# Rewriting a quantised feed-forward kernel: style fetch, roundings, statistics in pairs and the place of the x work

## The reference

```python
w = weights[conditions]                        # (32, 32, 32)
z = einsum('bct,bcd->bdt', x, w)               # style mixing of channels
def rmsnorm(x, g): return g * x * rsqrt(mean(x*x, -1) + 1e-8)
def act_quant(x):
    scale = 127 / clip(max(abs(x), -1), 1e-4)
    return clip(round(x * scale), -128, 127) / scale
def ternary(w):
    s = mean(abs(w))
    return round(tanh(w / (s + 1e-8))) * arctanh(s)
def linear(x, w, g): return act_quant(rmsnorm(x, g)) @ ternary(w).T
h = silu(linear(z, w1, g1)) * linear(z, w2, g2)     # 1024 hidden
out = x + linear(h, w3, g3)
```

## Time and profile before

| | |
|---|---|
| time, median of 3 runs | 78.19 us (77.08, 78.45, 78.19) |
| the profiled execution: span from first to last instruction | 76.6 us |
| what lies around the span, against the median | 1.6 us |
| DVE, POOL, PE, ACT busy | 58.1, 55.4, 48.0, 47.7 us |
| mean granted TensorE clock | 0.889 |

### The profile page before, as it was taken

How to read it: one execution, slowest core, us unless ns; L and a number is a source line. 1 busy time by engine, 2 the same in 40 slices (tenths; PEclk the granted TensorE clock), 3 DMA queues, 4 the chain that set the end, 5 groups by cost and what they waited for, 6 DMA issues and landing times.

```text
span 76.6 us, 1068 instructions
## 1 busy us (share of the span) xinstructions
PE 48.0 (63%) x298; PEld 31.3 (41%) x302; DVE 58.1 (76%) x117; ACT 47.7 (62%) x70; POOL 55.4 (72%) x97
## 2 busy tenths in 40 slices
...
GB/s 0 119 385 346 327 237 278 330 210 115 253 71 0 0 0 4 0 9 4 0 0 0 0 0 4 17 52 9 68 0 68 0 68 0 23 45 0 68 68 68
DMA packets 5369, 6.22 MB, mean 81 GB/s; under 512 B 500, under 2 KB 4980, under 8 KB 5364
## 3 DMA queue, kind: packets, MB, share of 16 engines
...
q0 software_dynamic: 256, 0.13, 0.8%
...
HBM read 5.11 MB, written 1.05 MB: 80 GB/s over the span
## 4 chain that ended last, share of the span: by engine, by line
DVE 24%; issue 22%; POOL 22%; DMA 12%; PE 11%; ACT 4%; SPq 0%; POOLq 0%; DVEq 0%
DMA w_sb<-in_L_ffn_w 12%; POOL hg L325 11%; PE y_ps L769 6%; DVE xg L477 6%; DVE cw_diag L446 5%; DVE x_peak L482 5%; PE a_ps L652 3%; PE t_ps L758 2%; POOL h_deq L302 2%; DVE hid L551 2%; ACT hr L413 2%; DVE abs_sum L438 2%; POOL h_root L316 2%; POOL h_base L311 2%; POOL h_base L309 1%
## 5 line engine op out<-in xcount | busy, mean ns | idle before, releaser
L325 POOL TENSOR_TENSOR hg<-hid,g_all 128x1024 f32<-128x1024 f32 x7 | 16.5, 2358 | 0.8 <-DVE hid L551 0.8
L413 ACT ACTIVATE hr<-hg,rounder,h_scale 128x1024 f32<-128x1024 f32 x7 | 8.7, 1241 | 5.5 <-DVE h_scale L574 5.5
L769 PE MATMUL y_ps<-w_t,hq_t 128*128 128x256 bf16 x64 | 10.3, 319 | 2.1 <-DVE hq_t L581 2.0
L560 DVE TENSOR_REDUCE h_peak<-hg 128x1 f32<-128x1024 f32 x8 | 9.7, 1217 | 1.7 <-POOL hg L325 1.6
L551 DVE SCALAR_TENSOR_TENSOR hid<-v_ps,x_deq,gate 128x1024 f32<-128x1024 f32 x8 | 10.2, 1271 | 0.9 <-PE v_ps L725 0.6
L725 PE MATMUL v_ps<-w_t,xq_t 128*128 128x512 bf16 x30 | 8.9, 415 | 3.0 <-DVE hid L551 2.9
L399 ACT ACTIVATE gate<-a_ps,x_deq 128x1024 f32<-128x1024 f32 x8 | 8.8, 1100 | 2.2 <-PE a_ps L725 2.1
L725 PE MATMUL a_ps<-w_t,xq_t 128*128 128x512 bf16 x30 | 8.7, 407 | 1.8 <-issue 1.3
L218 POOL DMA_INDIRECT cw_rows<-in_L_cond_weights,row_idx x8 | 7.9, 982 | 2.4 <-issue 2.1
L769 PEld LDWEIGHTS y_ps<-w_t,hq_t 128*128 128x128 bf16 x64 | 6.9, 115 | 5.6 <-DVE hq_t L581 4.1
L652 PE MATMUL a_ps<-x_sb,cw_diag 128*128 128x256 f32 x16 | 7.0, 597 | 2.5 <-DVE cw_diag L446 2.5
...
## 6 DMA issues: line engine op xcount, KB each, us to landing
...
cw_rows<-in_L_cond_weights,row_idx POOLq DMA_INDIRECT x8, 4.3
cond_i<-in_itok_B SPq DMA_DIRECT2D x1, 0.1 KB
```

Source lines behind the costliest of these rows:

```text
L325: pool.tensor_tensor(hg[:, b], hid[:, b], g3_all[:], ALU.mult).then_inc(hg_ready, 1)
L413: act.activation(hr[:, t % 2], hg[:, t % 2], ACT.Identity, scale=h_scale[:, t % 2:t % 2 + 1], bias=rounder[:]).then_inc(hr_ready, 1)
L560: dve.tensor_reduce(h_peak[:, b], hg[:, t % 2], AX.X, ALU.max, apply_absolute_value=True).then_inc(hpeak_ready, 1)
L769: last = pe.matmul(y_ps[t % 2][:, 0:FEAT], hq_t[:, t % 2, j, :], w_t[2][:, j, :], start=(j == 0), stop=(j == KH - 1))
```

## The change

Nearly every engine's list is written anew. By part:

- Style weights. SP reads the 32 style numbers into registers and issues, for each sequence, a transfer of its 32x32 matrix (4 KB) straight onto the diagonal of cw_diag: eight for each pair, between the loads of w3, x2, x3 and g3. The row numbers, gathers and diagonal copies go. DVE fills cw_diag with zeros. ACT issues the loads of w1, g12, w2 and x1 before its first arithmetic.
- Weight rounding. tanh and the rounding pass are one multiplication by 1/(2 arctanh(1/2) s), written to int16 (which rounds); the copy from PSUM clips to -1..1 (DVE) or takes the sign (ACT).
- Activation rounding. x and h are multiplied by the scale into int16 instead of adding a large number in float32; transposes read them dense, and the copies read int16 from PSUM.
- Statistics. eps comes in as an extra column of the squared tensor, so one power -0.5 gives the inverse root. For h, power, reciprocal, scale and factor are made for two tiles at once. hg has four buffers.
- x work. ACT copies the conditioned x from PSUM to SBUF (xc), DVE multiplies by g1 and POOL by g2. The x work of pairs 2 and 3, the transpose and copy of pair 1, and w3's rounding and turn stand behind the first silu. arctanh's steps move from POOL to DVE.
- The last tile's gain, rounding and copy are halved between two engines.

```diff
 @block.sync
+            load_x(sp, 0)
+            _, style = nc.values_load_multi_w_load_instructions(
+                cond.rearrange("(o b) -> o b", o=1), engines=[mybir.EngineType.SP], min_val=0, max_val=STYLES - 1,
...
+            def fetch(p):
+                for b in range(2 * p * PER_TILE, 2 * (p + 1) * PER_TILE):
+                    t, s = b // PER_TILE, slice(b % PER_TILE * CHAN, (b % PER_TILE + 1) * CHAN)
+                    sp.dma_start(cw_diag[s, t, s], cond_w[bass.ds(style[b], 1)].rearrange("o c d -> (o c) d")
+                                 ).then_inc(cw_in[p], 16)
+            sp.wait_ge(diag_zero, 1)
+            fetch(0)
+            load_w(sp, 2, 0)
+            fetch(1)
+            load_w(sp, 2, 1)
+            load_x(sp, 2)
+            fetch(2)
+            load_x(sp, 3)
+            fetch(3)
             sp.dma_start(g3_all[:], g3.partition_broadcast(P)).then_inc(g3_in, 16)
 @block.gpsimd
+            def x_gain(p):
+                pool.wait_ge(xc_copied, p + 1)
+                pool.tensor_tensor(xg[:, p, 1], xc[:, 2 * p:2 * p + 2, 0:FEAT],
+                                   g12[:, 1, :].unsqueeze(1).to_broadcast([P, 2, FEAT]), ALU.mult).then_inc(xg_p, 1)
+            def x_quant(p, k, i):
+                pool.wait_ge(xscale_ready, p + 1)
+                pool.tensor_scalar(xq[:, p, k, i], xg[:, p, k, i], x_scale[:, p, k, i:i + 1], 1.0,
+                                   ALU.mult, ALU.mult).then_inc(xq_done[p], 1)
+            def w_quantise(m, h):
+                pool.wait_ge(inv_ready, m + 1)
+                pool.tensor_scalar(half_of(m, h, w_q), half_of(m, h, w_sb), w_inv[:, m:m + 1], 1.0,
+                                   ALU.mult, ALU.mult).then_inc(w_quant[m][h], 1)
+            def inverse_rms(lo, hi):
+                pool.wait_ge(hss_ready, hi)
+                pool.tensor_tensor(h_rms[:, lo:hi], h_ss[:, lo:hi], neg_half[:, 0:hi - lo], ALU.pow
+                                   ).then_inc(hrms_ready, hi - lo)
```

More of the change, by code:

```diff
@@ L7 @@
 FP16 = mybir.dt.float16
[L8 to L9 removed]
+INT16 = mybir.dt.int16
 ALU = mybir.AluOpType
@@ L630, in _ @@
-            peak_of(last)
-            step_of(last)
-            scale_of(last)
-            rounding_last(last)
-            keep_h(last - 1)
-            residual(last - 2)
-            keep_h(last)
-            residual(last - 1)
-            residual(last)
+            abs_sum_half(0, 1)
+            mean(0)
+            w_quantise(0, 0)
+            w_quantise(0, 1)
+            keep_w(0, 0)
+            x_gain(0)
+            mean(1)
+            keep_w(0, 1)
+            x_peak_of(0)
+            x_scales(0)
@@ new lines, in _ @@
+            x_quant(0, 0, 0)
+            x_quant(0, 0, 1)
+            w_quantise(1, 0)
+            x_gain(1)
+            keep_w(1, 0)
+            x_keep(0)
+            mean(2)
+            arctanh_in()
+            x_peak_of(1)
+            x_scales(1)
+            arctanh_out()
+            hidden(0)
+            x_gain(2)
+            hidden(1)
+            x_keep(1)
+            peak_of(0)
+            x_peak_of(2)
+            x_scales(2)
+            hidden(2)
+            peak_of(1)
@@ new lines, in _ @@
+            scales(0, 2)
+            keep_w(2, 0)
+            x_gain(3)
+            hidden(3)
+            x_keep(2)
+            keep_h(0)
+            peak_of(2)
+            x_peak_of(3)
+            x_scales(3)
+            keep_h(1)
+            hidden(4)
+            residual(0)
+            x_keep(3)
+            peak_of(3)
+            scales(2, 4)
+            residual(1)
+            hidden(5)
+            keep_h(2)
+            peak_of(4)
+            keep_h(3)
+            hidden(6)
@@ L772, in _ @@
+                done.then_inc(y_ready, 1)
+            total(0)
+            pe.wait_ge(ident_made, 2)
+            condition(0)
+            w_turn(0, 0)
+            w_turn(0, 1)
+            total(1)
+            condition(1)
+            x_turn(0)
+            w_turn(1, 0)
+            w_turn(1, 1)
+            total(2)
             up_a(0)
             up_v(0)
-            x_turn(2)
-            x_turn(3)
-            for t in range(TILES):
-                if t + 1 < TILES:
-                    up_a(t + 1)
-                if t >= 3:
-                    down(t - 3)
-                if t + 1 < TILES:
-                    up_v(t + 1)
-                if t == 0:
-                    w_turn(2, 0)
-                    w_turn(2, 1)
-                if t >= 2:
-                    h_turn(t - 2)
```

875 lines of the change are left out of this document (407 added, 468 removed).

## The result

The changed kernel takes 94.78 us (median of four, 94.53 to 97.22) where the kernel before takes 78.0: a ratio of 1.227, with a 95% interval of 1.217 to 1.237. The forecast was 83.6 us in a range of 73.5 to 90. The direction was right and the size was not: it lies 4.8 us above the range. The profiled execution has a span of 92.8 us at a mean granted clock of 0.848; before it was 76.6 at 0.889, so 16.2 us came on top. Some executions of most kernels here take a few per cent longer than the rest, at a lower granted clock (97.22 us is one, at 0.833); the medians contain them, the ratios and intervals leave them out.

What follows compares the result with a forecast made beforehand. POOL was taken to bound the loop, 4.0 us a tile, with DVE 0.4 us behind. silu(0) at 28.4 plus 53.6 behind it gave 82.0 us of span; with 1.6 to the median, 83.6 us, range 73.5 to 90.

Steps and rivals of the forecast that it cites:

- Register reads: Ahead of silu(0), SP reads 32 style numbers into registers: 4.2 us taken, between 1.5 and 11.8.
- The chain from condition(0) to silu(0): Ahead of the loop: pair 0's transfers land at 10.2 us, then steps in written order, silu(0) at 28.4.
- In-order lists: Loop: x_turn(2) ahead of up_v(2) idles DVE 3.7 us before hidden(2); a second stall, 2.4 us, at residual(0).
- Rival 1: Loop: the walked stalls are filled and DVE's own work bounds; 74.0 us, chance 0.25.
- rival 2: Half of the packing: hidden(2) at 10.5 us after silu(0), prologue at 27.7; some 77.5 us, chance 0.10.
- The port: DVE and POOL exclude each other with two SBUF inputs: nothing taken for small operands or x_gain, 2.4 us at worst.
- a row with x_step beside a POOL pow: Kernel before: x_step, with two small SBUF inputs, ran its 0.15 us without a pause; small operands priced at nothing.
- TensorE's clock: Loop with long waits may get the lower level, 1.2 GHz, doubling some ten steps of 0.6 to 0.9 us.
- rival 3: Registers at 11.8 us or slower TensorE, either adding 7.6: 91 us; chance 0.15 together with slow int16 reads.
- Durations: Instruction times: ACT's rounding 1.15 us, int16 PSUM copies 0.68, DVE's weights 0.75, x_quant 0.47, gain 2.36, POOL's x_gain 1.18.
- Rival 4: DVE reads int16 PSUM at the reduce's rate, 8 us more: 88 to 92 us; chance within a shared 0.15.
- Chances: Whole kernel: faster by over 2% 0.24, within 2% 0.13, slower 0.63.

Runs made afterwards that it cites:

- the three parts together: Changed kernel with registers read in four portions, h's scale by per-partition pointer, and x_turns and x_quants behind what the current tile needs: 86.9 us, ratio 1.127.
- The best order tried for the new lists: Changed kernel with the x work back ahead of hidden(0), registers read in four portions and h's scale by pointer: 85.84 us, ratio 1.119.

## Why the prediction was wrong, by its steps

The sum was 82.0 us of span; it was 92.8. Of the 10.8 us, 5.6 lie ahead of silu(0) (33.98 for 28.4) and 5.2 behind it (58.8 for 53.6). The steps that failed are three terms: the reads, taken at 4.2 us, took 10.07; the lock on h's scale, taken at nothing, took 2.2; and TensorE's lower clock, left out of the walk, took some 3. The direction came from the lists' order, and that step held.

- **Register reads: the largest step that failed.** They were taken at 4.2 us, between 1.5 and 11.8, and took 10.07; the transfers of pair 0, forecast to land at 10.2, let condition(0) start at 16.32. With no transfer beside them they take 4.27 us; that this is so near the 4.2 is luck, as the middle of two guesses 8 times apart. What was left out is that other transfers run just then, 2 MB of weights among them; no such interaction is in the sum, though the upper end of the bounds held. Missing too is the read of the array's address, 1.71 us of the 10.07. The Trainium skill, page "Runtime: NRT & Kernel Launch", section "Instruction fetch mechanics", gives some 200 ns a register: measured were 0.13 without other transfers and 0.31 with them, on either side of it (0.10 and 0.25 without the address).
- **The chain from condition(0) to silu(0)** was walked at 18.2 us and took 17.7. Right.
- **In-order lists: right, and the core of the forecast's direction.** x_turn(2) ahead of up_v(2) gave 3.70 us of idle DVE in front of hidden(2) (3.7 forecast), 14.15 us after silu(0) (13.2), and the second stall came at residual(0). That order decides was then shown by moving only names in the lists: 7.1 us, of which the clock's part was not measured by itself. Rival 1 (packed) and rival 2 (half) are out by this.
- **The port: taken at nothing, with 2.4 us at worst.** The first scale of h took 2.35 us in place of 0.16, the third (78.75 us) 0.57, and hidden(3) started 20.4 us after silu(0) and not 17.4; of these 3.0 us 0.95 were there at hidden(2), the other 2.05 are the lock. I had let a row with x_step beside a POOL pow speak for small operands in general. It speaks for no more than that pair of instructions. In the changed kernel a pow meets the lock too: the one at 53.89, begun 0.11 us behind DVE's x_gain, took 1.13 us and not 0.70. The Trainium skill, page "SBUF — State Buffer", section "Who interferes with whom", states the rule without an exception for small operands, and beside a gain the trace agrees with it (2.35 us).
- **TensorE's clock: in rival 3, with 15% for three things together, and outside the forecast.** Between 48 and 63 us the granted clock is 0.67 and up_a takes 1.86 us at the lower level of 1.2 GHz, where the same four matmuls take 1.02 at 40.65. In front of it TensorE had waited 5.13 us, and the granted clock fell in that wait, at 54.4. That moves keep_h(0) by a further 1.4 us and residual(0) by 1.7 (x_turn 1.04, up_a 1.91 and down 1.49 in a row, where 0.6, 0.9 and 0.9 were forecast). The rest, from residual(0) to the end, was shorter than walked by some 0.9 us (24.2 for 25.0): 0.95 + 2.05 + 1.4 + 1.7 - 0.9 = 5.2. The clock was low behind both stalls: I had forecast both, and should have run the steps behind them at the lower level, in the forecast itself. No run changed the clock alone, so its share rests on these durations.
- **Durations.** An issue with a register address 0.50 us (3.88 for eight), and 0.47 with a fixed one (3.77 for eight in the kernel without the reads, once the first loads are out): the address adds next to nothing. ACT's rounding 1.14 (1.15 forecast), copies from int16 PSUM 0.68 (0.68), DVE's weights 0.75 (0.75), x_quant 0.48 (0.47), gain 2.35: right. Rival 4 is out. POOL's x_gain took 1.43 in the mean and not 1.18.
- **Chances.** 0.63 on slower was right. The range stopped at 90 because late reads, the port and the clock were priced as alternatives, each by itself; all three came, and the last is not independent of the others, as the clock fell around the waits.

What is not settled: why eight numbers took 4.48 us to read at the start and 0.9 later with the DMA engines as busy; and where the other half of the loss lies. Of the 16.2 us of span the three parts together gave back 7.4 to 8.2. The best order tried for the new lists is still 11.9% above the kernel before, and how much of that the x work itself costs no run tells.
